# The order of two gates, and which semaphore wait rides on an instruction, in a 256-step recurrence

## The chip, the cores and the metric

The kernel runs on one core of one Trainium2 chip, in one launch. The metric is the time of an execution on the device in microseconds. Five engines work beside each other, each through its own queue: TensorE (PE, with its weight loads shown as PEld), VectorE (DVE), ScalarE (ACT), GpSimd (POOL) and SyncE (SP). They meet at semaphores only.

## The reference, cut to what matters

The model is a stack of small layers on an image of 2 x 16 x 16 positions with 64 channels: a neighbourhood attention, an attention behind a group norm, a windowed attention, a mixture of experts, a causal attention, and at the end a recurrence of the LSTM kind over the 256 positions of each image. Only the recurrence is touched by the change:

```
def step(carry, xs):
    h, c = carry
    xi_t, xf_t, xg_t, xo_t = xs
    i_t = jax.nn.sigmoid(xi_t + h @ V_i)
    g_t = jnp.tanh(xg_t + h @ V_c)
    o_t = jax.nn.sigmoid(xo_t + h @ V_o)
    c_new = h * c + i_t * g_t
    h_new = o_t * jnp.tanh(c_new)
    return ((h_new, c_new), h_new)
```

Each step needs the hidden state h of the step before. The cell's old value is multiplied by h, so there is no forget gate to compute. The two images' 64 channels fill the 128 partitions, and the state is one column of 128 numbers.

## The kernel before, in words

The program is written by hand, one function per engine; the order of the work on an engine is the order in which its function writes it, and `wait_ge` and `then_inc` on named semaphores (`on("name")`) are all that orders the engines among each other. Waits written ahead of an instruction, several of them at times, are given to it by the builder.

Everything ahead of the recurrence is left aside here: the loads of all weights, layers 0 to 3, and the split of the recurrent weights into two 16-bit parts (`vparts`, part 0 the leading bits, part 1 the rest). The recurrence is a loop of 16 iterations on ScalarE, TensorE and VectorE (lines 363, 666 and 925), with 16 steps written out in each body; `u` is the step in the body, `t` the step overall. Sums of gates lie in PSUM, in banks 0 to 2 for eight steps and in banks 3 to 5 for the next eight, one column per step: `bank[pre]` for g, `bank[pre + 1]` for i, `bank[pre + 2]` for o.

One step:

- TensorE (lines 667 to 684) waits for `ha_ready`, and adds the weight parts times `ha` for two gates, four matmuls of one column, through the helper `recur` (line 658, whose instructions are shown at line 659). It waits for `hb_ready`, adds the leading weight part times `hb` for the i gate (signals `i_pre`) and the g gate (signals `g_pre`), and then does the three matmuls of the o gate (signals `o_pre`). Together ha and hb are the hidden state in two 16-bit parts. In six of eight steps one more matmul, the helper `b_part` (line 467, shown at 468) or `x_part` (line 654, shown at 655), prepares the other set of banks with the bias or the input part.
- ScalarE (lines 365 to 381) waits for `cell_ready` (line 366, the cell of the step before has been read and written) and `i_pre` (line 367), and takes the sigmoid of i into `gi` in SBUF (line 368). It waits for `g_pre` (line 369) and takes the tanh of g into `gt`, which lies in PSUM bank 6 (line 370, signals `gates`). It waits for `o_pre` and takes the sigmoid of o three times over into `go` (line 374, signals `o_gate`). It waits, where u is 0, for `grid_set` (line 377), then for `gates` (line 378) and `hc_ready` (line 379), and does tanh(gi * gt + hc) into `tc` (line 380, signals `tanh_c`), which is the tanh of the new cell.
- VectorE (lines 926 to 943) waits for `o_gate` and negates o (line 930), waits for `tanh_c` and forms ha (`terms_a`, line 933, signals `ha_ready`), then hb (`terms_b`, line 936, signals `hb_ready`), then the new `cell` (line 939, signals `cell_ready`), the output column `hs` (line 941) and `hc`, the hidden state times the cell (line 943, signals `hc_ready`).

Of the kernel before, what the change touches and what calls it, by code (L numbers as in the profile page):

```python
# [17 lines left out]
ACT = mybir.ActivationFunctionType  # L18
# [21 lines left out]
PRE = HSCALE * VSCALE  # L40
# [32 lines left out]
def build(nc, x, const, bands, later, vec, positions, w0, w1, w2, w3, w4, w5, out):  # L73
    with ExitStack() as ctx:
        def sb(name, shape, dt=F32):
            return ctx.enter_context(nc.sbuf_tensor(name, shape, dt))
# [3 lines left out]
        def on(name):  # L80

            if name not in semaphores:
                semaphores[name] = ctx.enter_context(nc.semaphore("s_" + name))
            return semaphores[name]

        bank = [ctx.enter_context(nc.psum_tensor(f"bank{i}", [P, 512], F32)) for i in range(8)]
# [93 lines left out]
        gi, go = sb("gi", [P, 1]), sb("go", [P, 2, 4])  # L180
        terms_a, terms_b = sb("terms_a", [P, 2, 3]), sb("terms_b", [P, 2, 4])
        cell, hc = sb("cell", [P, 1]), sb("hc", [P, 1])
        ha, hb = sb("ha", [P, 1], F16), sb("hb", [P, 1], F16)
# [11 lines left out]
        gt, tq = bank[6][:, 0:1], bank[7][:, 0:4]  # L195
# [58 lines left out]
        def _(act):  # L254
# [108 lines left out]
            with act.Fori(0, N, STEPS_IN_BODY) as base:  # L363
                for u in range(STEPS_IN_BODY):
                    t, pre, at, two = base + u, (u // CHUNK) * 3, u % CHUNK, u % 2
                    act.wait_ge(on("cell_ready"), t + 1)
                    act.wait_ge(on("i_pre"), t + 1)  # L367
                    act.activation(gi[:], bank[pre + 1][:, at:at + 1], ACT.Sigmoid, scale=1.0 / PRE)  # L368
                    act.wait_ge(on("g_pre"), t + 1)
                    act.activation(gt, bank[pre][:, at:at + 1], ACT.Tanh, scale=1.0 / PRE)\  # L370
                       .then_inc(on("gates"), 1)
                    act.wait_ge(on("o_pre"), t + 1)

                    act.activation(go[:, two, 0:3], bank[pre + 2][:, at:at + 1].broadcast_to([P, 3]), ACT.Sigmoid,  # L374
                                   scale=1.0 / PRE).then_inc(on("o_gate"), 1)
                    if u == 0:
                        act.wait_ge(on("grid_set"), 2)
                    act.wait_ge(on("gates"), t + 1)
                    act.wait_ge(on("hc_ready"), t + 1)
                    act.activation(tc_ends, gt.broadcast_to([P, 2]), ACT.Tanh, scale=gi[:],  # L380
                                   bias=hc[:]).then_inc(on("tanh_c"), 1)

        @block.tensor
        def _(pe):
# [19 lines left out]
            for qt in range(HALVES):  # L404
                for ch in range(2):
                    at = KROW0[qt] * SIDE + ch * KCH
# [60 lines left out]
            def b_part(parity, k):  # L467
                return mm(bank[3 * parity + k][:, 0:CHUNK], w5s[:, (6 + k) * P:(7 + k) * P], ones[:],  # L468
                          start=True, stop=False, skip_group_check=True)
# [142 lines left out]
            for h in range(HALVES):  # L612
                for b in range(B):
                    u, at = h * B + b, b * N + h * P
# [39 lines left out]
            def x_part(parity, k, start):  # L654
                return mm(bank[3 * parity + k][:, 0:CHUNK], w5s[:, k * P:(k + 1) * P], x5[:, bass.ds(start, CHUNK)],  # L655
                          start=False, stop=False, skip_group_check=True)

            def recur(parity, k, at, part, h):
                return mm(bank[3 * parity + k][:, at:at + 1], vparts[:, part, k], h, start=False, stop=False,  # L659
                          skip_group_check=True)  # L660
# [5 lines left out]
            with pe.Fori(0, N, STEPS_IN_BODY) as base:  # L666
                for u in range(STEPS_IN_BODY):
                    t, parity, at = base + u, u // CHUNK, u % CHUNK
                    pe.wait_ge(on("ha_ready"), t + 1)
                    for k in (1, 0):  # L670
                        for part in range(2):
                            recur(parity, k, at, part, ha[:])

                    pe.wait_ge(on("hb_ready"), t + 1)
                    recur(parity, 1, at, 0, hb[:]).then_inc(on("i_pre"), 1)
                    recur(parity, 0, at, 0, hb[:]).then_inc(on("g_pre"), 1)
                    for part in range(2):
                        recur(parity, 2, at, part, ha[:])
                    recur(parity, 2, at, 0, hb[:]).then_inc(on("o_pre"), 1)

                    if at < 3:
                        b_part(1 - parity, at)
                    elif at < 6:
                        x_part(1 - parity, at - 3, base + (parity + 1) * CHUNK)
# [380 lines left out]
```

## Time and profile before

| what | value |
|---|---|
| median of 3 runs | 447.81 us (445.8 to 448.85) |
| the profiled execution's own time | 448.33 us |
| its span, first to last instruction | 446.5 us |
| TensorE, weight loads, VectorE, ScalarE, GpSimd busy | 290.3, 222.9, 261.2, 210.9, 21.0 us |
| mean granted TensorE clock | 0.635 of full speed |

The span is what the profile shows of the one execution that was profiled; its own time holds 1.8 us more around it. Busy times are sums over instructions, and instructions of one engine that overlap count once. ACTq is ScalarE's sequencer: instructions of its own that only wait stand under that name. "issue" in a chain of waits is time in which an engine waited for nothing that the profile shows.

### The profile page before, as it was taken

The numbers are of one execution on the slowest core, as the hardware profiler recorded it, in microseconds if no ns is written. First come the engines' busy times: TensorE is split into PE (matmuls) and PEld (weight loads), VectorE is DVE, ScalarE is ACT, GpSimd is POOL, SyncE is SP. The second block draws the span as 40 slices with busy tenths as digits, with TensorE's granted clock in tenths as the row PEclk, the third lists the DMA queues.
The fourth block names the chain that finished last, engine by engine and source line by source line (L and its number), as shares of the span: only waits on it lengthen the run. The fifth ranks groups of instructions, "written<-read, shape, count | busy, mean of one in ns | idle before, by whom it ended". The sixth has DMA issues, their size and how long they took to land.

```text
span 446.5 us, 11853 instructions
## 1 busy us (share of the span) xinstructions
PE 290.3 (65%) x3273; PEld 222.9 (50%) x3273; DVE 261.2 (59%) x2309; ACT 210.9 (47%) x1169; POOL 21.0 (5%) x38
## 2 busy tenths in 40 slices
PE   1899889989855555555555555555555555555553
PEld 1466447643545555544555555544555555445552
DVE  0976454655356666666666666666666666666664
ACT  1488352253544444444444444444444444444442
POOL 6920000000000000000000000000000000000000
PEclk9999999799975555555555555555555555555555
DMA  8400000000000000000000000000000000000000
GB/s 305 188 3 0 1 0 2 0 1 0 0 3 2 0 0 0 0 0 0 0 0 0 0 0 0 0 0 0 0 0 0 0 0 0 0 0 0 0 0 12
DMA packets 2828, 5.78 MB, mean 13 GB/s; under 512 B 1408, under 2 KB 1792, under 8 KB 2816
## 3 DMA queue, kind: packets, MB, share of 16 engines
q1 hardware_dynamic: 2384, 4.55, 2.7%
q10 hardware_dynamic: 432, 1.08, 0.6%
q8 instruction: 6, 0.10, 0.1%
q14 instruction: 6, 0.05, 0.0%
HBM read 5.50 MB, written 0.13 MB: 13 GB/s over the span
## 4 chain that ended last, share of the span: by engine, by line
ACT 36%; PE 35%; DVE 14%; issue 11%; DMA 1%; ACTq 1%; SPq 0%; DVEq 0%
PE bank L659 18%; ACT bank L380 16%; ACT go L374 11%; ACT gi L368 6%; DVE ha L933 6%; DVE terms_a L933 4%; PE bank L439 2%; PE bank L419 2%; PE bank L391 2%; PE bank L428 2%; DMA cst<-in_const 1%; PE bank L591 1%; PE bank L552 1%; PE bank L603 1%; ACTq L367 1%
## 5 line engine op out<-in xcount | busy, mean ns | idle before, releaser
L659 PE MATMUL bank<-ha,vparts 128*128 128x1 f16 x1536 | 95.5, 169 | 133.3 <-DVE ha L933 133.3
L659 PEld LDWEIGHTS bank<-ha,vparts 128*128 128x128 f16 x1536 | 74.7, 106 | 156.1 <-DVE ha L933 156.1
L368 ACT ACTIVATE gi<-bank 128x1 f32<-128x1 f32 x256 | 43.8, 171 | 167.4 <-PE bank L659 167.4
L930 DVE TENSOR_SCALAR go<-go 128x1 f32<-128x1 f32 x256 | 39.3, 153 | 86.5 <-ACT go L374 86.5
L380 ACT ACTIVATE bank<-bank,hc,gi 128x2 f32<-128x2 f32 x256 | 83.2, 325 | 0.0
L659 PE MATMUL bank<-hb,vparts 128*128 128x1 f16 x768 | 69.5, 165 | 0.0
L933 DVE CUSTOM_DVE_ANT_0 terms_a<-bank,go 128x3 f32<-128x3 f32 x256 | 41.1, 161 | 30.4 <-ACT bank L380 2.1
L655 PE MATMUL bank<-x,w5s 128*128 (+1 forms) x198 | 55.7, 357 | 0.2 <-DVE x L769 0.2
L468 PE MATMUL bank<-ones,w5s 128*128 128x8 f32 x198 | 55.4, 354 | 0.0
L939 DVE SCALAR_TENSOR_TENSOR cell<-bank,gi,hc 128x1 f32<-128x1 f32 x256 | 54.9, 214 | 0.0
L659 PEld LDWEIGHTS bank<-hb,vparts 128*128 128x128 f16 x768 | 53.9, 104 | 0.0
L374 ACT ACTIVATE go<-bank 128x3 f32<-128x3 f32 x256 | 52.2, 204 | 0.0
L655 PEld LDWEIGHTS bank<-x,w5s 128*128 128x128 f32 x198 | 48.8, 307 | 0.6 <-issue 0.6
L468 PEld LDWEIGHTS bank<-ones,w5s 128*128 128x128 f32 x198 | 48.6, 304 | 0.1
L943 DVE TENSOR_TENSOR hc<-hs,cell 128x1 f32<-128x1 f32 x256 | 40.8, 159 | 8.8
L370 ACT ACTIVATE bank<-bank 128x1 f32<-128x1 f32 x256 | 42.8, 167 | 0.0
L936 DVE CUSTOM_DVE_ANT_0 terms_b<-bank,go 128x4 f32<-128x4 f32 x256 | 40.0, 156 | 0.0
L941 DVE TENSOR_TENSOR hs<-bank,go 128x1 f32 x256 | 38.4, 150 | 0.0
L936 DVE DVE_READ_ACCUMULATOR2_ANT hb<- 128x1 f16 x256 | 21.8, 85 | 0.0
L933 DVE DVE_READ_ACCUMULATOR2_ANT ha<- 128x1 f16 x256 | 21.7, 85 | 0.0
L391 PE MATMUL bank<-blank 128*128 128x512 bf16 x77 | 21.4, 389 | 0.0
L284 ACT ACTIVATE pr<-sc,nmx 128x176 f32<-128x176 f32 x32 | 13.8, 433 | 4.8 <-DVE nmx L725 4.8
(215 smaller groups left out, 303.0 us busy)
## 6 DMA issues: line engine op xcount, KB each, us to landing
w3s<-in_w SPq DMA_DIRECT2D x1, 804.0 KB, 11.1
ltr<-in_later SPq DMA_DIRECT2D x1, 709.0 KB, 9.4
bias<-in_positions ACTq DMA_DIRECT2D x1, 704.0 KB, 6.9
bias<-in_positions SPq DMA_DIRECT2D x1, 704.0 KB, 8.1
w2s<-in_w SPq DMA_DIRECT2D x1, 640.0 KB, 10.4
w5s<-in_w SPq DMA_DIRECT2D x1, 576.0 KB, 11.8
w0s<-in_w ACTq DMA_DIRECT2D x1, 336.0 KB, 3.9
w1s<-in_w SPq DMA_DIRECT2D x1, 256.0 KB, 9.4
```

The lines of the kernel that those rows point to most:

```text
L368: act.activation(gi[:], bank[pre + 1][:, at:at + 1], ACT.Sigmoid, scale=1.0 / PRE)
L370: act.activation(gt, bank[pre][:, at:at + 1], ACT.Tanh, scale=1.0 / PRE)\
L374: act.activation(go[:, two, 0:3], bank[pre + 2][:, at:at + 1].broadcast_to([P, 3]), ACT.Sigmoid, scale=1.0 / PRE).then_inc(on("o_gate"), 1)
L380: act.activation(tc_ends, gt.broadcast_to([P, 2]), ACT.Tanh, scale=gi[:], bias=hc[:]).then_inc(on("tanh_c"), 1)
L468: return mm(bank[3 * parity + k][:, 0:CHUNK], w5s[:, (6 + k) * P:(7 + k) * P], ones[:], start=True, stop=False, skip_group_check=True)
L655: return mm(bank[3 * parity + k][:, 0:CHUNK], w5s[:, k * P:(k + 1) * P], x5[:, bass.ds(start, CHUNK)], start=False, stop=False, skip_group ...
L659: return mm(bank[3 * parity + k][:, at:at + 1], vparts[:, part, k], h, start=False, stop=False, skip_group_check=True)
L930: ts(go[:, two, 3:4], o, -1.0, None, ALU.mult).then_inc(on("minus_o"), 1)
L933: dve.tensor_tensor_reduce(terms_a[:, two], tq[:, 0:3], go[:, two, 0:3], HSCALE, 0.0, ALU.mult, ALU.add, ha[:]).then_inc(on("ha_ready"), 1)
L936: dve.tensor_tensor_reduce(terms_b[:, two], tq, go[:, two], -HSCALE, 0.0, ALU.mult, ALU.add, hb[:]).then_inc(on("hb_ready"), 1)
L939: stt(out=cell[:], in0=gt, scalar=gi[:], in1=hc[:], op0=ALU.mult, op1=ALU.add)\
L943: tt(hc[:], hs[:, bass.ds(t, 1)], cell[:], ALU.mult).then_inc(on("hc_ready"), 1)
```

## The change

On ScalarE the tanh of g comes first and the sigmoid of i second; ahead of the first stands the wait for `g_pre`, written before the one for `cell_ready`; ahead of the second the wait for `i_pre`; the semaphore `gates` is incremented by the second. On TensorE the g gate's matmuls come before those of the i gate, both with ha and with hb.

```diff
                 for u in range(STEPS_IN_BODY):
                     t, pre, at, two = base + u, (u // CHUNK) * 3, u % CHUNK, u % 2
+                    act.wait_ge(on("g_pre"), t + 1)
                     act.wait_ge(on("cell_ready"), t + 1)
+                    act.activation(gt, bank[pre][:, at:at + 1], ACT.Tanh, scale=1.0 / PRE)
                     act.wait_ge(on("i_pre"), t + 1)
-                    act.activation(gi[:], bank[pre + 1][:, at:at + 1], ACT.Sigmoid, scale=1.0 / PRE)
-                    act.wait_ge(on("g_pre"), t + 1)
-                    act.activation(gt, bank[pre][:, at:at + 1], ACT.Tanh, scale=1.0 / PRE)\
+                    act.activation(gi[:], bank[pre + 1][:, at:at + 1], ACT.Sigmoid, scale=1.0 / PRE)\
                        .then_inc(on("gates"), 1)
                     act.wait_ge(on("o_pre"), t + 1)
...
                     pe.wait_ge(on("ha_ready"), t + 1)
-                    for k in (1, 0):
+                    for k in (0, 1):
                         for part in range(2):
                             recur(parity, k, at, part, ha[:])
 
                     pe.wait_ge(on("hb_ready"), t + 1)
+                    recur(parity, 0, at, 0, hb[:]).then_inc(on("g_pre"), 1)
                     recur(parity, 1, at, 0, hb[:]).then_inc(on("i_pre"), 1)
-                    recur(parity, 0, at, 0, hb[:]).then_inc(on("g_pre"), 1)
                     for part in range(2):
                         recur(parity, 2, at, part, ha[:])
                     recur(parity, 2, at, 0, hb[:]).then_inc(on("o_pre"), 1)
```

## Rows read from the trace of the kernel before

**Rows 1.** The page: busy us by engine, and the granted clock in 40 slices

```profile
PE 290.3 (65%) x3273; PEld 222.9 (50%) x3273; DVE 261.2 (59%) x2309; ACT 210.9 (47%) x1169; POOL 21.0 (5%) x38
...
PEclk9999999799975555555555555555555555555555
```

**Rows 2.** Stretches: length, busy us (and instructions) by engine, clock, DMA, GB/s

```profile
0.00:123.50 123.50, 104.93 (x594) 60.81 (x594) 65.47 (x258) 58.72 (x148) 21.00 (x38) 0.97 0.12 45
123.50:442.00 318.50, 184.63 (x2677) 161.81 (x2677) 194.24 (x2042) 152.19 (x1022) 0.00 (x0) 0.51 0.00 0
```

**Rows 3.** The page: the chain that ended last, by line

```profile
PE bank L659 18%; ACT bank L380 16%; ACT go L374 11%; ACT gi L368 6%; DVE ha L933 6%; DVE terms_a L933 4%; PE bank L439 2%; PE bank L419 2%; PE bank L391 2%; PE bank L428 2%; DMA cst<-in_const 1%; PE bank L591 1%; PE bank L552 1%; PE bank L
```

**Rows 4.** Timeline of one step: start us, length us, engine, line, operation [idle before]

```profile
301.15 0.21 DVE L939 SCALAR_TENSOR_TENSOR cell<-bank,gi,hc 128x1 f32<-128x1 f32 x1
...
301.21 0.27 PE L659 MATMUL bank<-ha,vparts 128*128 128x1 f16 x4 [0.84 <-DVE ha L933]
...
301.34 0.19 PE L659 MATMUL bank<-hb,vparts 128*128 128x1 f16 x2
...
301.47 0.16 DVE L943 TENSOR_TENSOR hc<-hs,cell 128x1 f32<-128x1 f32 x1
301.60 0.17 ACT L368 ACTIVATE gi<-bank 128x1 f32<-128x1 f32 x1 [0.65 <-PE bank L659]
301.67 0.17 ACT L370 ACTIVATE bank<-bank 128x1 f32<-128x1 f32 x1
301.72 0.20 ACT L374 ACTIVATE go<-bank 128x3 f32<-128x3 f32 x1
301.87 0.33 ACT L380 ACTIVATE bank<-bank,hc,gi 128x2 f32<-128x2 f32 x1
...
302.23 0.16 DVE L933 CUSTOM_DVE_ANT_0 terms_a<-bank,go 128x3 f32<-128x3 f32 x1
```

**Rows 5.** The chain of waits through the same step: start us, length us, what

```profile
301.52 0.02 issue
301.54 0.02 ACTq L367
301.56 0.04 issue
...
302.21 0.02 issue
```

**Rows 6.** Lines 367, 379 and 380 alone: count, ns min/median/max, first and last start

```profile
L367 ACTq EVENT_SEMAPHORE  x256: 17/17/17, 123.2 to 441.3; - x128
...
L379 ACTq EVENT_SEMAPHORE  x256: 17/17/187, 123.3 to 441.5; - x128
...
L380 ACT ACTIVATE bank<-bank,hc,gi x256: 325/325/326, 123.5 to 441.6; 128x2 f32<-128x2 f32 x128
```

**Rows 7.** Timeline of ScalarE in a step with u = 0

```profile
302.92 0.17 ACT L370 ACTIVATE bank<-bank 128x1 f32<-128x1 f32 x1
...
303.17 0.33 ACT L380 ACTIVATE bank<-bank,hc,gi 128x2 f32<-128x2 f32 x1
```

**Rows 8.** Groups by line, 200 to 400 us: count, busy us, mean ns, idle before

```profile
L659 PE MATMUL bank<-hb,vparts 128*128 128x1 f16 x482 | 43.7, 165 | 0.0
...
L368 ACT ACTIVATE gi<-bank 128x1 f32<-128x1 f32 x160 | 27.4, 171 | 104.4 <-PE bank L659 104.4
L370 ACT ACTIVATE bank<-bank 128x1 f32<-128x1 f32 x160 | 26.7, 167 | 0.0
```

**Rows 9.** Timeline of ScalarE: the tanh in two early steps

```profile
124.76 0.33 ACT L380 ACTIVATE bank<-bank,hc,gi 128x2 f32<-128x2 f32 x1
...
125.99 0.33 ACT L380 ACTIVATE bank<-bank,hc,gi 128x2 f32<-128x2 f32 x1
```

**Rows 10.** Stretches at the recurrence's start, columns as in rows 2

```profile
123.50:125.00 1.50, 0.61 (x11) 0.52 (x11) 0.92 (x9) 0.86 (x6) 0.00 (x0) 1.00 0.02 5
...
127.50:130.00 2.50, 1.67 (x22) 1.49 (x22) 1.52 (x16) 1.20 (x9) 0.00 (x0) 0.50 0.00 0
```

## The prediction

> **What bounds the kernel now.** I read the totals first. No engine is busy for more than 65% of the span of 446.5 us, and the granted clock of TensorE stands at half from the thirteenth slice to the end [rows 1]. The table of stretches then splits the span: everything ahead of the recurrence takes 123.5 us, the recurrence 318.5 us [rows 2], and 4.5 us are left. In the recurrence TensorE is busy for 184.6 us of 318.5, VectorE for 194.2, ScalarE for 152.2, so no engine fills it: it is one dependent chain, walked once per step. The chain of waits says the same: its largest lines are 659 (the recurrent matmuls), 380 (tanh of the cell), 374, 368 and 933, which are all in the step [rows 3]. So I need the period and the order of one step. The last tanh of a step runs 256 times, first at 123.5 and last at 441.6 us [rows 6]: (441.6 - 123.5) / 255 = 1.247 us per step.
>
> One step in order of time [rows 4]: TensorE starts on ha at 301.21 and on hb at 301.34; ScalarE starts the i gate at 301.60, the g gate at 301.67, the o gate at 301.72 and the tanh at 301.87; VectorE's next product (terms_a) starts at 302.23, and so on. The reader is to see that ScalarE's instructions overlap (0.07 and 0.05 us from start to start, though each lasts 0.17) and that ScalarE idles 0.65 us until TensorE's sums come. Everything from the i gate's sum to the tanh is on the path, 301.52 to 301.87.
>
> **What the step pays for a wait.** In the chain of waits, TensorE's part ends at 301.52; then 0.02 of issue, 0.02 of a separate wait instruction at line 367, 0.04 of issue, and the i gate at 301.60 [rows 5]. Line 367 is the wait for i_pre, the second of two that are written ahead of the gate. It stands 256 times as an instruction of its own on ScalarE's queue [rows 6], one a step, and none stands at line 366 (cell_ready) beside it: the wait written first rides on the instruction, the later ones go into one instruction ahead of it. What a riding wait costs is in the same chain: between the tanh's end and terms_a's start, one wait, lie 0.02, from 302.21 [rows 5]. And the kernel shows both ways at one place. In 15 of 16 steps the wait for `gates` is written first ahead of the tanh: the g gate starts at 301.67, the tanh at 301.87, 0.20 later [rows 4]. Where u = 0, the wait for grid_set is written first and `gates` falls to the separate instruction (this is the 0.19 long one at line 379 [rows 6]): g gate at 302.92, tanh at 303.17, 0.25 later [rows 7]. So standing apart costs 0.05 there, and 0.06 by the pieces at line 367 (0.08 against 0.02).
>
> **The change, part by part.** (1) The waits of the first gate. After the change g_pre is written first and cell_ready second, so g_pre rides on the g gate and cell_ready stands apart. The count of instructions stays the same. The separate wait is for the `cell` that VectorE begins at 301.15 and ends at 301.36 [rows 4]; with the 0.08 of its own path the g gate could start at 301.45, and the sum lets it start at 301.52 + 0.02 = 301.54. The new separate wait hides behind TensorE with 0.09 to spare; without that cover it would cost what line 367 costs now. Gain: 301.60 - 301.54 = 0.06. Bounds: 0.05 (the tanh's two forms) and 0.06; a gate may also turn out to gain nothing from the riding form, which I keep as a rival.
>
> (2) The order of the gates on ScalarE. The tanh waits for whichever of g and i is second. Now that is g, 0.07 behind i; afterwards it is i, behind g. What does the second gate wait for? Its own sum: TensorE's two hb matmuls lie 0.03 apart (0.19 for two of 0.165 each [rows 4, 8]), so its riding wait clears about 0.03 after the first one's, and ScalarE's own pace decides. Two rows give that pace: i to g is 0.07, g to o is 0.05 [rows 4]. The second is the nearer row: in it the g gate (Tanh, PSUM to PSUM) leads and a Sigmoid that writes SBUF follows, the very pair that g and i will be. I take 0.05 and keep 0.07 as the other end, for it may belong to the first pair after an idle stretch whatever the functions are; 0.03, the sums alone, is the end below. The i gate lasts 0.171 against 0.167 for g [rows 8], which loses 0.004. So: g 301.54, i 301.59, its end 301.76, then the 0.03 that lie between the g gate's end (301.67 + 0.17) and the tanh now, and the tanh starts at 301.79 to 301.80 instead of 301.87. Gain of both parts: 0.07 a step; 0.054 with the 0.07 spacing; about 0.09 with 0.03.
>
> (3) The order on TensorE. The same nine matmuls of the same shapes stand in the step, two names are swapped, and the one that signals first now signals g_pre. Cost nothing, for the sum and the order of arrival are the same with g and i exchanged; nothing is queued past. The x_part and b_part matmuls behind the step stay where they are; a step without them has TensorE idle for 0.84 us ahead of ha [rows 4], the mean step with them for (318.5 - 184.6) / 256 = 0.52 [rows 2], against the 0.07 by which the step shortens.
>
> (4) What could be late next. The tanh also needs hc_ready: hc starts at 301.47 and ends at 301.63 [rows 4]; with 0.08 for a separate wait that allows a tanh at 301.71, still 0.08 ahead of 301.79. It hangs on the same tanh of the step before as the sums do, so the distance stays as the step shrinks. The o gate follows i by 0.05 to 0.07, at 301.64 to 301.66 instead of 301.72; it isn't in the way of the tanh, and VectorE's negation of o moves ahead with it. The `u = 0` step keeps its separate wait for `gates`, now signalled by the i gate, and gains the same.
>
> **Sum.** 256 steps x 0.070 us = 17.9 us. From the profiled execution's 448.33 us (446.5 of span and 1.8 around it) this gives 430.4; the median of the three runs shown is 447.81, 0.5 lower, so 429.9, which I give as 430.
>
> Against the spacing of 0.07 and 0.05 from start to start in part (2), which rows 4 show, stands a rule of the Trainium skill: "ScalarE: Activation LUTs", section "What ACT_TABLE_LOAD costs", has an ACTIVATE at 186 ns plus 0.833 per element and lets neighbours overlap by about 93 ns, which would put the i gate 94 ns behind g. By that rule the tanh would start near 301.83 and the estimate would be some 9 us of gain. This case's trace disagrees [rows 4].
>
> **Rivals.**
> A. The i gate keeps the 0.07 spacing. For it: 0.07 is what the first pair of a step shows now. Against: that pair has Sigmoid first. 256 x 0.054 = 13.8: 434.0.
> B. The second gate starts only when half of the first has run (0.09 behind). The tanh comes at 301.83, gain 0.035 to 0.04, some 9 us: 439. Against it stand both spacings in every step.
> C. The riding form gains nothing, or g_pre is not the wait that rides. Then the g gate stays at 301.60 and only the order acts: with 0.05 spacing 0.012 gained, 3 us, 445; with 0.07 and the longer i gate 0.004 lost, 1 us, 449. For it: no row shows a ScalarE instruction riding on a TensorE sum that is late. Against: lines 367 and 379 agree on 0.05 to 0.06.
> D. Slower: the i gate, whose wait clears after g has begun, is not taken into the pipeline and starts only when g has ended. Then g 301.54, i 301.71, end 301.88, tanh 301.91: 0.045 later than now, 256 x 0.045 = 11.5 us, 459. It decides as soon as the second gate starts more than 0.12 to 0.13 behind the first. Against it: the tanh itself clears its wait while the o gate is running (301.72 to 301.92) and starts at 301.87, inside it [rows 4].
> E. TensorE's clock rises with the shorter step. At the start of the recurrence it is granted fully (2.4 GHz), right after the busy stretch, and is at half (1.2 GHz) from 127.5 us on [rows 10]; two tanhs of those first steps are 1.23 apart [rows 9] against 1.247 later. It would give 256 x 0.017 = 4.4 us more: 425.6. Against: the step stays as sparse as it is, 58% busy now and some 61% then.
>
> **How the numbers follow.** The forecast has 0.62, A 0.18, B 0.05, C 0.07, D 0.03, E 0.05. The range runs from 426.5 to 437: it holds the forecast, A, the lower wait cost (0.05 with the 0.07 spacing, 0.045 a step, 11.5 us: 436.3) and most of what a spacing of 0.03 could give, and leaves out C, D, most of B and E. Faster by over 1% (about what a measurement of this kernel tells from no change) are the forecast, A, B and E: 0.90. Within 1% is C: 0.07. Slower is D: 0.03.
>
> **What would show it.** The separate wait, cell_ready's now and again at line 367, starts over 0.1 us ahead of the sums' end and is gone from the chain of waits, in which g (line 368) follows TensorE's end by 0.02; g to i is 0.05; the first gate to the tanh is 0.25 to 0.26 (now 0.27, i to tanh); the tanh's 256 starts lie 1.177 us apart; everything ahead of 123.5 us is unmoved. A g gate at 0.08 behind the sum means C, a second gate 0.07 behind means A, 0.12 or more D, and a granted clock over 0.6 in the loop E. If the gate-to-tanh distance shrank but the period did not, another wait, hc_ready or cell_ready, would have taken the place, and the prediction would be wrong.

## The result, and the profile after

The changed kernel takes 432.5 us (431.78 to 433.3) against 447.4 us for the kernel before, measured beside it: a ratio of 0.9685, 95% interval 0.9652 to 0.9718. The forecast was 430 in a range from 426.5 to 437; the gain is 14.9 us where 17.9 were forecast.

First the totals, to see what moved at all. The page of the changed kernel, busy time by engine and the granted clock, beside [rows 1]:

```profile
PE 290.7 (67%) x3268; PEld 223.6 (52%) x3273; DVE 261.5 (61%) x2309; ACT 210.9 (49%) x1169; POOL 21.0 (5%) x38
...
PEclk9999999689995555555555555555555555555555
```

Every engine does the work that it did, to 0.7 us; only the shares rose, since the span fell from 446.5 to 431.5 us. The clock stands at half in the recurrence as before. Where the span went shows the group of the last tanh of a step, lines 367 and 380 of the changed kernel alone, beside [rows 6] (count, ns min/median/max, first and last start):

```profile
L367 ACTq EVENT_SEMAPHORE  x256: 17/17/17, 121.0 to 426.2; - x128
```

```profile
L380 ACT ACTIVATE bank<-bank,hc,gi x256: 325/325/326, 124.1 to 426.6; 128x2 f32<-128x2 f32 x128
```

From first to last tanh it is 426.6 - 124.1 = 302.5 us, and was 441.6 - 123.5 = 318.1: the recurrence gained 15.6 us, 0.061 a step, 1.186 us each against 1.247. The stretch ahead of it, which the change doesn't touch, came out 0.6 us longer in this execution. I call the length from first to last tanh the length of the recurrence below: it is the sharper measure, for the stretch ahead of it took between 118.6 and 124.1 us in the profiles of this study, whatever the kernel.

Line 367 has its 256 waits again, but it is another wait, for cell_ready. Its first start (121.0) lies 3.1 us ahead of the first tanh, where i_pre's lay 0.3 ahead of it; that is the first step alone, whose cell is set to zero ahead of the loop. What counts is a step in the middle. Line 367 alone, from 301.5 to 301.76 us:

```profile
L367 ACTq EVENT_SEMAPHORE  x1: 17/17/17, 301.6 to 301.6; - x1
```

Whether it still costs something is read from the chain of waits through the same step of the changed kernel, beside [rows 5] (start us, length us, what):

```profile
301.43 0.30 PE bank L659 x5
301.73 0.02 issue
301.75 0.16 ACT bank L368
301.91 0.09 ACT gi L370
302.00 0.02 issue
302.02 0.33 ACT bank L380
```

ACTq is gone from it: the wait at 301.6 is over before TensorE's part ends at 301.73. Between the end of the sum and the first gate lie 0.02 us of issue, where 0.02 of issue, 0.02 of ACTq and 0.04 of issue stood. The same step in the timeline of ScalarE, beside [rows 4]:

```profile
301.75 0.16 ACT L368 ACTIVATE bank<-bank 128x1 f32<-128x1 f32 x1 [0.59 <-PE bank L659]
301.82 0.17 ACT L370 ACTIVATE gi<-bank 128x1 f32<-128x1 f32 x1
301.87 0.18 ACT L374 ACTIVATE go<-bank 128x3 f32<-128x3 f32 x1
302.02 0.33 ACT L380 ACTIVATE bank<-bank,hc,gi 128x2 f32<-128x2 f32 x1
```

The reader is to see what did not change: 0.07, 0.05 and 0.15 us from start to start, 0.27 from the first gate to the tanh, exactly as with i in front. ScalarE's idle time ahead of the first gate fell from 0.65 to 0.59, and that 0.06 is the whole of the gain. By groups, 200 to 400 us, beside [rows 8], the gates' lengths (mean ns behind the busy us):

```profile
L374 ACT ACTIVATE go<-bank 128x3 f32<-128x3 f32 x168 | 30.4, 181 | 0.0
L370 ACT ACTIVATE gi<-bank 128x1 f32<-128x1 f32 x168 | 28.1, 167 | 0.0
...
L368 ACT ACTIVATE bank<-bank 128x1 f32<-128x1 f32 x168 | 26.2, 156 | 99.3 <-PE bank L659 99.3
```

The second gate lasts 167 ns, whichever it is; i in first place took 171, g in first place takes 156. The o gate is third in both kernels, and went from 204 ns (0.20 in [rows 4]) to 181.

### The profile page after: what moved, and what is told of

It is laid out like the page before. It is cut to its first block, busy times and chain, and to the rows that moved or that the text cites. A ratio compares the mean times of both kernels' runs of the same rounds, so it can differ in the third digit from the quotient of the medians.

```text
span 431.5 us, 11848 instructions
## 1 busy us (share of the span) xinstructions
PE 290.7 (67%) x3268; PEld 223.6 (52%) x3273; DVE 261.5 (61%) x2309; ACT 210.9 (49%) x1169; POOL 21.0 (5%) x38
## 4 chain that ended last, share of the span: by engine, by line
PE 37%; ACT 37%; DVE 15%; issue 8%; DMA 2%; SPq 0%; ACTq 0%; DVEq 0%
ACT bank L380 19%; PE bank L659 18%; ACT bank L368 8%; DVE ha L933 6%; ACT go L374 5%; DVE terms_a L933 4%; ACT gi L370 2%; PE bank L591 2%; PE bank L439 2%; PE bank L419 2%; PE bank L428 2%; DMA cst<-in_const 2%; PE bank L391 1%; PE bank L603 1%; PE bank L552 1%
## 5 line engine op out<-in xcount | busy, mean ns | idle before, releaser
L368 ACT ACTIVATE bank<-bank 128x1 f32<-128x1 f32 x256 | 39.9, 156 | 151.8 <-PE bank L659 151.8
L374 ACT ACTIVATE go<-bank 128x3 f32<-128x3 f32 x256 | 46.3, 181 | 0.0
L370 ACT ACTIVATE gi<-bank 128x1 f32<-128x1 f32 x256 | 42.8, 167 | 0.0
L391 PE MATMUL bank<-blank 128*128 128x512 bf16 x72 | 20.1, 386 | 0.6 <-issue 0.5
L284 ACT ACTIVATE pr<-sc,nmx 128x176 f32<-128x176 f32 x32 | 13.8, 433 | 4.5 <-DVE nmx L725 4.3
## 6 DMA issues: line engine op xcount, KB each, us to landing
w2s<-in_w SPq DMA_DIRECT2D x1, 640.0 KB, 10.6
```

## The experiments

Two theories stood after the result. W: the gain is the wait that rides on the first gate, and the order of the gates gives nothing. O: the order of the gates, on ScalarE or on TensorE, gives part of it.

**Only the wait.** The kernel before, with two lines exchanged:

```diff
-act.wait_ge(on("cell_ready"), t + 1)
 act.wait_ge(on("i_pre"), t + 1)
+act.wait_ge(on("cell_ready"), t + 1)
 act.activation(gi[:], bank[pre + 1][:, at:at + 1], ACT.Sigmoid, scale=1.0 / PRE)
```

> The kernel before with one edit: ahead of the i gate the wait for i_pre is written first and the one for cell_ready second; the gates and the matmuls keep the old order. Theory W (the whole gain is the wait that rides): 432.5 us, as the changed kernel, a period of 1.186 us, i gate about 0.02 behind the end of its sum, and 0.27 from the i gate to the tanh as in both kernels. Rival O (the order of the gates gives part of it, because what ends last then is the i gate): 434 to 436 us.

Measured: 430.51 us (430.36 to 431.51) against 447.0, ratio 0.9641 (0.9609 to 0.9673). The group of line 380 in this kernel:

```profile
L380 ACT ACTIVATE bank<-bank,hc,gi x256: 325/325/326, 121.2 to 423.7; 128x2 f32<-128x2 f32 x128
```

302.5 us from first to last tanh, the changed kernel's length to the digit. The 2 us between the two times are in the stretch ahead, which took 121.2 us here and 124.1 there.

**Only the order.** The changed kernel with cell_ready written first again, so that g_pre stands apart:

```diff
-act.wait_ge(on("g_pre"), t + 1)
 act.wait_ge(on("cell_ready"), t + 1)
+act.wait_ge(on("g_pre"), t + 1)
 act.activation(gt, bank[pre][:, at:at + 1], ACT.Tanh, scale=1.0 / PRE)
```

> The changed kernel with one edit undone: the wait for cell_ready is written first again, so that the wait for g_pre stands apart. Theory W: as the kernel before, 447.4 us, a period of 1.247 us, 0.08 from the sum's end to the g gate. Rival O: 1 to 3 us faster than before.

Measured: 446.68 us (445.45 to 449.23) against 447.0, ratio 1.0004 (0.9976 to 1.0032). Its chain of waits, from the end of TensorE's part to the g gate:

```profile
301.38 0.02 issue
301.40 0.02 ACTq L367
301.42 0.04 issue
301.46 0.10 ACT bank L368
```

The same three pieces as in [rows 5], with the gates exchanged. First and last tanh start at 120.6 and 439.1 us, 318.5 us apart. The two halves of the change are told apart by this pair of runs: the wait alone gives 15.6 us, the order alone nothing.

**Both once more, side by side.** The 2 us between the changed kernel and the run with only the wait were explained by the stretch ahead on one profile each, so both ran again on one chip.

> The changed kernel once more, on the same chip as the next two. Theory: what lay between it and the run with only the wait's order changed (432.5 against 430.5 us) is the stretch ahead of the recurrence (124.1 against 121.2 us in the two profiles), not the order of the gates: the two agree within 0.3% here, and the tanh's first and last start lie 302.5 us apart again.

> The kernel before with i_pre's wait written first, once more. Theory: as the changed kernel within 0.3%, recurrence 302.5 us. Rival (the order of the gates costs 1 to 2 us): 0.3 to 0.5% faster than the changed kernel in this call too.

Measured, five rounds: 430.81 us (429.16 to 432.38), ratio 0.9648 (0.9613 to 0.9684), and 429.63 us (428.57 to 432.31), ratio 0.9645 (0.961 to 0.968). The first pair of numbers is the changed kernel, the second the one with only the wait. The ratios differ by 0.0003 and the medians by 0.3%; the lengths of the recurrence are 425.5 - 122.6 = 302.9 and 421.9 - 118.6 = 303.3 us, so the shorter time has the longer recurrence, and the stretch ahead makes the difference once more. A length scatters by up to 0.8 us among profiles of the same kernel (302.5 and 303.3 with only the wait), and the order is worth nothing that can be measured.

**Which sum the path goes through.** The changed kernel with TensorE's old order, while ScalarE takes g first:

```diff
-for k in (0, 1):
+for k in (1, 0):
...
-recur(parity, 0, at, 0, hb[:]).then_inc(on("g_pre"), 1)
 recur(parity, 1, at, 0, hb[:]).then_inc(on("i_pre"), 1)
+recur(parity, 0, at, 0, hb[:]).then_inc(on("g_pre"), 1)
```

> The changed kernel with TensorE's old order: i first, g second, while ScalarE still wants g first. Theory: the path goes through the sum of the gate that ScalarE takes first, which now comes one matmul later, 0.026 us: 432.5 + 256 x 0.026 = 439.2 us, period 1.21 us. Rival (the tanh's start is set by the second gate alone, whose sum is early enough either way): 432.5 us.

Measured: 438.9 us (438.75 to 439.86) against 447.0, ratio 0.9828 (0.9795 to 0.986). The length is 432.2 - 120.4 = 311.8 us, 9.3 more than the changed kernel's, where one matmul later was expected to cost 6.7. That the time fell on the expected 439.2 is luck: the stretch ahead was 3.7 us shorter in this profile (120.4 against 124.1) and hid the rest. Its chain has a sixth matmul in it, and g starts 0.02 behind it:

```profile
300.75 0.34 PE bank L659 x6
301.09 0.02 issue
301.11 0.10 ACT bank L368
```

So the two orders must agree, though neither is better: with both old or both new the first gate waits for five matmuls (0.30 to 0.31), with TensorE's old order under ScalarE's new one for six (0.34). The opposite mixture, ScalarE's old order over TensorE's new one, wasn't run. It costs 9.3 / 255 = 0.036 a step, a little more than the 0.026 from matmul to matmul. The excess lies in TensorE's part of the chain, for behind it the distances are the old ones; its cause is open.

**The first gate's sum one matmul sooner.** If the path is the arrival of the first gate's sum and fixed distances behind it, making that sum earlier must pay in full:

```diff
-for k in (0, 1):
-    for part in range(2):
-        recur(parity, k, at, part, ha[:])
+for k, part in ((0, 0), (0, 1), (1, 0)):
+    recur(parity, k, at, part, ha[:])
...
 recur(parity, 0, at, 0, hb[:]).then_inc(on("g_pre"), 1)
+recur(parity, 1, at, 1, ha[:])
 recur(parity, 1, at, 0, hb[:]).then_inc(on("i_pre"), 1)
```

> The changed kernel with g's hb matmul moved ahead of the second ha matmul of i, so that g_pre comes after four matmuls, not five; i_pre comes as before. Theory: g starts 0.026 us earlier, i follows at 0.068 behind it (its sum is there by then), the tanh comes 0.026 earlier: 432.5 - 6.7 = 425.8 us, period 1.16 us. Rival 1 (hb isn't ready at that place, TensorE stands for it): 429 to 432.5 us. Rival 2 (the i gate's sum sets the tanh): 432.5 us.

Measured: 424.93 us (424.81 to 425.02) against 447.0, ratio 0.9509 (0.948 to 0.9538). The length is 418.2 - 121.7 = 296.5 us, 6.0 less than the changed kernel's, against 6.7 expected, which is within the scatter of lengths. The chain and the timeline of ScalarE in this kernel:

```profile
301.37 0.28 PE bank L659 x4
301.65 0.02 issue
301.67 0.16 ACT bank L368
```

```profile
301.67 0.16 ACT L368 ACTIVATE bank<-bank 128x1 f32<-128x1 f32 x1 [0.57 <-PE bank L659]
301.74 0.17 ACT L370 ACTIVATE gi<-bank 128x1 f32<-128x1 f32 x1
301.81 0.17 ACT L374 ACTIVATE go<-bank 128x3 f32<-128x3 f32 x1
301.94 0.33 ACT L380 ACTIVATE bank<-bank,hc,gi 128x2 f32<-128x2 f32 x1
```

Four matmuls instead of five, and the first gate to the tanh still 0.27. The o gate is later against g (0.14 behind it, was 0.12), since its sum was not moved; the tanh doesn't mind, since it waits for g and i but not for o.

**What sets 0.07 and 0.05.** This is where the forecast's sum was off: it took 0.05 between g and i. The first rival explanation was the function:

```diff
-act.activation(gt, bank[pre][:, at:at + 1], ACT.Tanh, scale=1.0 / PRE)
+act.activation(gt, bank[pre][:, at:at + 1], ACT.Sigmoid, scale=1.0 / PRE)
```

> The changed kernel with Sigmoid in place of Tanh for g, so that all three gates are the same function (g's values are changed by it, the work is not). Theory P (the distance from the first gate to the second is 0.068 us by its place after an idle stretch): 0.068 and 0.051 between the starts as before, period 1.186 us. Rival F (the distance goes by the functions of the pair): one of the two distances changes, most likely the first to 0.051, and the period falls to 1.17 us.

Measured in one execution: 429.56 us against 445.88, length 422.9 - 120.4 = 302.5. (This version computes another g, so its numbers are of use for the time alone.) The timeline of ScalarE in this kernel:

```profile
300.41 0.16 ACT L368 ACTIVATE bank<-bank 128x1 f32<-128x1 f32 x1 [0.59 <-PE bank L659]
300.48 0.17 ACT L370 ACTIVATE gi<-bank 128x1 f32<-128x1 f32 x1
300.53 0.18 ACT L374 ACTIVATE go<-bank 128x3 f32<-128x3 f32 x1
```

0.07 and 0.05 with one function throughout: the function has no part in it. The second explanation was where the leading gate writes; g moved from PSUM to SBUF:

```diff
-gt, tq = bank[6][:, 0:1], bank[7][:, 0:4]
+gt, tq = sb("gts", [P, 1])[:], bank[7][:, 0:4]
```

> The changed kernel with the tanh of g in SBUF, not in PSUM. Theory P: 0.068 from g to i stays, period 1.186 us, 432.5 us, save for what the reads of the final tanh and of VectorE change. Rival D (the distance goes by where the leading gate writes): it changes by some 0.01 to 0.02 us, and the time by 2.5 to 5 us.

Measured: 438.03 us (436.72 to 438.75) against 445.88, ratio 0.9799 (0.9746 to 0.9851). The timeline of ScalarE and the group of line 380:

```profile
300.44 0.17 ACT L368 ACTIVATE gts<-bank 128x1 f32<-128x1 f32 x1 [0.59 <-PE bank L659]
300.51 0.17 ACT L370 ACTIVATE gi<-bank 128x1 f32<-128x1 f32 x1
300.56 0.18 ACT L374 ACTIVATE go<-bank 128x3 f32<-128x3 f32 x1
300.71 0.35 ACT L380 ACTIVATE bank<-gts,hc,gi 128x2 f32<-128x2 f32 x1
```

```profile
L380 ACT ACTIVATE bank<-gts,hc,gi x256: 355/356/356, 122.0 to 432.0; 128x2 f32<-128x2 f32 x128
```

The distances stay once more, so the place of the output has no part in them either. The time went up for another reason, which the expectation left open as "save for": the last tanh lasts 356 ns instead of 325 with its input in SBUF, 0.030 x 256 = 7.7 us, and the length is 310.0, 7.5 more.

The third explanation is the place in line: the first pair of a step has 0.07, the later ones 0.05. One more instruction ahead of g:

```diff
+act.activation(extra[:], bank[pre][:, at:at + 1], ACT.Tanh, scale=1.0 / PRE)
 act.activation(gt, bank[pre][:, at:at + 1], ACT.Tanh, scale=1.0 / PRE)
```

> The changed kernel with one more instruction ahead of the g gate: the tanh of the same sum into a spare column in SBUF, on which the wait for g_pre now rides. Theory P: the spare one starts where g did, g follows 0.068 later and i 0.051 behind g; the tanh comes 0.051 later, period 1.237 us, 445.5 us. Rival F, or a distance that goes by where the leading one writes: g to i keeps 0.068, the tanh comes 0.068 later, period 1.254 us, 450 us.

Measured in one execution: 456.08 us against 445.88, length 449.2 - 122.5 = 326.7. The timeline of ScalarE in this kernel, whose lines stand one or two lower:

```profile
301.50 0.17 ACT L369 ACTIVATE extra<-bank 128x1 f32<-128x1 f32 x1 [0.59 <-PE bank L661]
301.57 0.17 ACT L370 ACTIVATE bank<-bank 128x1 f32<-128x1 f32 x1
301.62 0.20 ACT L372 ACTIVATE gi<-bank 128x1 f32<-128x1 f32 x1
301.67 0.19 ACT L376 ACTIVATE go<-bank 128x3 f32<-128x3 f32 x1
301.86 0.33 ACT L382 ACTIVATE bank<-bank,hc,gi 128x2 f32<-128x2 f32 x1
```

The distances are the ones of theory P: 0.07 from the first to the second, and then 0.05, also from g to i. But both expected times were missed, theory P's 445.5 by 10.6 us and the rival's 450 by 6.1. The i gate, now in third place, lasts 0.20 us and not 0.167; with the 0.05 it delays the tanh to 0.36 behind the first instruction, 0.09 more than 0.27. That is 256 x 0.09 = 23 us of the 24.2 by which the length grew. So the distance goes by the place. g has no wait of its own here, and still starts 0.07 behind the first, so a wait on the second instruction isn't what makes it 0.07. Whether the idle time ahead of the first one makes it was not varied: every step has it.

The length of a gate does not go by its place alone, though it is tempting to read this run so. The o gate was third in the kernel before (0.20 us), where g, which writes PSUM, stands ahead of it, and is third in the changed kernel (181 ns), where i, which writes SBUF, stands ahead. The 0.20 us of the i gate here has g ahead of it again. So in these traces the third instruction is long where the second writes PSUM, with one column (i) or three (o). No run varied that alone, and the cause stays open.

**Is the wait for cell_ready free where it stands now?** With g in SBUF and two columns each for g and i it guards nothing and was taken out:

```diff
-act.wait_ge(on("cell_ready"), t + 1)
+gt, gi = gt2[:, two:two + 1], gi2[:, two:two + 1]
```

> The kernel with g in SBUF, and with two columns for g and for i that alternate by step, so that nothing is left for cell_ready to guard, and with that wait taken out of ScalarE. Theory (the separate wait for cell_ready is hidden behind TensorE's sums, 0.09 us ahead): the same time and period as the run with g in SBUF alone, within 0.3%. Rival (a separate wait costs something on ScalarE's queue even when its event is past): up to 0.06 a step, 15 us, faster.

Measured: 438.5 us (436.88 to 440.48) against 438.03 for the run with g in SBUF alone, and its first and last tanh start at 122.0 and 432.0 as in that one. There is no wait instruction at line 367 in this trace at all, so the 256 that stand there otherwise cost nothing: their event is past before the sum comes.

**The same edit where `gates` stands apart.** On top of the kernel with g's hb matmul moved:

```diff
+act.wait_ge(on("gates"), t + 1)
 if u == 0:
     act.wait_ge(on("grid_set"), 2)
-act.wait_ge(on("gates"), t + 1)
```

> The kernel with g's hb matmul moved forward, and in the step with u = 0 the wait for gates written ahead of the one for grid_set, so that it rides on the tanh there too. Theory: 0.05 us gained in each of 16 steps, 0.8 us in all: 424.1 us, and u = 0 steps as long as the others (1.16 us). Rival: no gain, 424.9 us.

Measured, five rounds: 422.88 us (422.52 to 423.28) against 446.16, ratio 0.9469 (0.9442 to 0.9496). Its length is 416.3 - 120.6 = 295.7 us, 0.8 less than without the edit. That is the 0.8 expected, but no more than the scatter of lengths noted above, and of the 2.0 us between the two medians 1.1 lie in the stretch ahead (121.7 and 120.6 in the profiles). What tells more is line 379 alone, first in the kernel without the edit and then in the one with it:

```profile
L379 ACTq EVENT_SEMAPHORE  x256: 17/17/138, 121.6 to 418.1; - x128
```

```profile
L379 ACTq EVENT_SEMAPHORE  x256: 17/17/38, 120.4 to 416.2; - x128
```

The long waits of the u = 0 steps are gone. What that is worth shows the timeline of ScalarE in a step with u = 0 of the kernel without the edit:

```profile
307.47 0.16 ACT L368 ACTIVATE bank<-bank 128x1 f32<-128x1 f32 x1 [0.57 <-PE bank L659]
...
307.79 0.33 ACT L380 ACTIVATE bank<-bank,hc,gi 128x2 f32<-128x2 f32 x1
```

There the tanh comes 0.32 behind the first gate, in the 15 other steps 0.27; with the edit it is 0.27 in every step. So the price of standing apart is 0.05 here too, and 16 x 0.05 is the 0.8 us.

> g's hb matmul forward and gates' wait riding in the u = 0 step, once more beside the other two: recurrence 295.8 us, 6.7 us less than the changed kernel's, and the time 6.7 us below it.

Measured beside the two repeats: 423.76 us (420.51 to 426.37) against 445.49, ratio 0.9483 (0.9426 to 0.9539), length 418.1 - 122.3 = 295.8; the changed kernel took 430.81 there, 7.1 more. This is the fastest version of the study, some 5% below the kernel before.

## Why the prediction was right, and where it was off

**What bounds the kernel, and the price of a wait: right.** Part (1) said that the wait written first rides, that a wait standing apart costs 0.05 to 0.06 us where its event comes last, and that cell_ready's would be hidden. The chain after the change, the run with the wait alone (15.6 us, 0.061 a step) and the run without cell_ready's wait show each of the three. Rival C, that the riding form gains nothing on a late sum of TensorE's, fell with the run that had the wait alone.

**The order on ScalarE: the step that failed.** Part (2) took 0.05 between g and i, because the pair g and o was "the nearer row". It measured 0.07: the distance belongs to the first pair of a step, as rival A had it, and neither to the function nor to the output's memory. That is 0.017 x 256 = 4.4 us of gain that didn't come. A small part came back from a term of the opposite sign: i in second place lasts 167 ns, not the 171 that it had in first place, 1.0 us. That makes 17.9 - 4.4 + 1.0 = 14.5 us, and 15.6 were measured; the other 1.1 are rounding of the rows, which have two digits (the riding wait is worth 0.061 a step by the run with the wait alone, where the sum had 0.06 or a little less), and scatter of the lengths. By mechanism it was rival A that came true; its 13.8 us were 1.8 short for the same reasons, the 1.0 among them. The time fell into the range because the range had been drawn to hold A. By the prediction's own sign, a second gate 0.07 behind, it is A as well. Part (2) as a whole was worth nothing, as the run with the order alone says. Rivals B and D, larger distances, were not seen, and E neither: the clock is at half from slice 13 on, before and after.

**The order on TensorE: right, with a condition.** Part (3) put it at nothing, as g and i exchange their parts. The run with TensorE's old order under ScalarE's new one shows that this needs both engines to agree; without it 9.3 us of the gain are lost by the length of the recurrence (6.4 by the medians, 438.9 against 432.5, with a shorter stretch ahead).

**What is late next: right.** hc_ready had 0.08 to spare by part (4) and cell_ready 0.09 by part (1). Even a step of 295.7 / 255 = 1.160 us, 0.087 shorter than before (the fastest version), met neither: the first gate to the tanh is 0.27 there as well, and the wait instructions at lines 367 and 379 last 17 ns in the median.

**From the length to the time.** 15.6 us of the recurrence became 15.0 of the span and 14.9 of the medians, since the stretch ahead of it came out longer. The change doesn't touch that stretch, which took 118.6 to 124.1 us among the profiles; its scatter belongs in the range of a forecast of this kernel. What it comes from wasn't looked into.

## What to carry to other kernels

In a chain that is walked hundreds of times, find for each instruction on it the wait whose event comes last, and write that one first, so that it rides on the instruction (with this builder, which gives the first wait to the instruction and the others to one ahead of it); the others may stand apart, as cell_ready's does here, as long as their events are past before the last one comes. Before two independent operations are exchanged, ask whether the distance between them belongs to the operations or to their places in line: here it was the place, and the exchange gave nothing. What did pay, beside the wait, was the earlier arrival of the first one's sum, so the producer should finish the one that the consumer takes first, and only then go on with the other.

## What the runs showed that I had not expected

- On ScalarE the start-to-start distance of the gates goes by their place in the step: 0.07 us for the first pair, which follows an idle stretch of 0.57 to 0.65, and 0.05 for later ones whose sum is there, with different functions, outputs and numbers of instructions.
- The length of a gate goes by its place and by more than that. In second place it lasted 167 ns in every kernel; in first place 156 with its output in PSUM and 171 in SBUF, be it a sigmoid or a tanh; in third place 0.20 us behind a gate that writes PSUM and 181 ns behind one that writes SBUF (173 where it started 0.07 and not 0.05 behind it). So one more instruction ahead of the one that is waited for cost 0.09 us in the order tried, not its 0.05 of distance.
- The last tanh of a step, whose scale and bias are a column each in SBUF, takes 325 ns with its input in PSUM and 356 in SBUF: moving one column of 128 numbers between the memories cost 7.5 us over 256 steps.
